# Cross-attention and experts, two layers: x stays in SBUF, the experts' outputs are added to it by one accumulating transfer per group

## What is computed

```python
# layer 0 (all matrices float32)
x = x + tanh(g_xattn[0]) * attention0(layernorm(x), ctx, mask)     # 16 heads of 8
n = layernorm(x)
e = argmax(n @ Wg.T)                                               # one of 8 experts
y = gelu(n @ W1[e] + b1[e]) @ W2[e] + b2[e]                        # 128 -> 512 -> 128
x = x + tanh(g_ffn[0]) * y
# layer 1
x = x + tanh(g_xattn[1]) * attention1(layernorm(x), ctx)           # no mask
x = x + tanh(g_ffn[1]) * top2_of_16_experts(layernorm(x))          # capacity 8 per sequence
```

## Time and profile before

| | us |
|---|---|
| median of 3 runs | 517.33 |
| lowest and highest | 516.51 and 517.77 |
| the profiled execution: time | 514.45 |
| the profiled execution: span from first to last instruction | 512.4 |

### The profile page before, as it was taken

How to read it: one execution, slowest core, us unless ns; L and a number is a source line. 1 busy time by engine, 2 the same in 40 slices (tenths; PEclk the granted TensorE clock), 3 DMA queues, 4 the chain that set the end, 5 groups by cost and what they waited for, 6 DMA issues and landing times.

```text
span 512.4 us, 21949 instructions
## 1 busy us (share of the span) xinstructions
PE 443.6 (87%) x8481; PEld 324.1 (63%) x8481; DVE 349.9 (68%) x883; ACT 320.6 (63%) x764; POOL 272.6 (53%) x325
## 2 busy tenths in 40 slices
PE   2789999999988796999998799998998697779996
PEld 1456676666655685999973466666665565445554
DVE  5578778888768665545532678888898677644545
ACT  2355566666865873677744466777777377685653
POOL 2622634646466178888886445553545236534454
PEclk9999999999999998999999799999999899898999
DMA  7124444232111155565436000110031000000112
GB/s 209 51 55 130 98 127 125 82 95 70 44 55 35 35 139 90 82 89 71 44 35 155 2 25 24 45 35 24 4 95 26 21 4 3 2 2 5 42 53 68
DMA packets 50629, 30.69 MB, mean 60 GB/s; under 512 B 12384, under 2 KB 46944, under 8 KB 50528
## 3 DMA queue, kind: packets, MB, share of 16 engines
q1 hardware_dynamic: 37072, 18.54, 13.7%
q0 software_dynamic: 6640, 4.67, 7.2%
q10 hardware_dynamic: 6816, 6.08, 4.3%
HBM read 19.42 MB, written 9.85 MB: 57 GB/s over the span
## 4 chain that ended last, share of the span: by engine, by line
PE 49%; DVE 20%; issue 13%; ACT 7%; POOL 4%; DMA 3%; ACTq 1%; DVEq 1%; SPq 0%; POOLq 0%
PE T_ps L865 8%; DVE maxes L600 7%; PE S_ps L854 6%; DVE prob L608 4%; PE A_ps L880 4%; PE f_H_ps L1199 3%; PE m_H_ps L1458 3%; PE f_Y_ps L1213 3%; PE S_ps L848 3%; PE Q_ps L835 2%; PE m_X_ps L1485 2%; PE m_T_ps L1498 2%; PE Q_ps L747 2%; PE m_X_ps L1469 2%; PE X_ps L897 2%
## 5 line engine op out<-in xcount | busy, mean ns | idle before, releaser
L600 DVE TENSOR_REDUCE maxes<-S_ps 128x16 f32<-128x1024 f32 x64 | 78.2, 1222 | 49.1 <-PE S_ps L854 49.0
L428 POOL TENSOR_TENSOR k_blk<-kT,col_a 128x512 f32<-128x512 f32 x64 | 67.7, 1067 | 79.4 <-ACT kT L489 54.0
L531 ACT ACTIVATE probT<-T_ps 128x512 f32<-128x512 f32 x128 | 76.0, 594 | 46.4 <-PE T_ps L865 45.6
L865 PE MATMUL T_ps<-col_a,prob 128*128 128x128 f32 x512 | 83.8, 287 | 15.1 <-DVE prob L608 11.3
L865 PEld LDWEIGHTS T_ps<-col_a,prob 128*128 128x128 f32 x512 | 56.5, 143 | 55.4 <-issue 29.9
L608 DVE TENSOR_TENSOR prob<-S_ps,maxes 128x512 f32<-128x512 f32 x128 | 82.5, 686 | 2.2
L1147 POOL DMA_INDIRECT x_mid<-f_out,f_rows x39 | 60.9, 1562 | 11.9 <-issue 9.2
L880 PE MATMUL A_ps<-v_blk,probT 128*32 128x18 f32 x4096 | 48.8, 187 | 0.1
L1012 DVE TENSOR_TENSOR f_hid<-f_H_ps,f_b 128x512 f32<-128x512 f32 x39 | 27.0, 692 | 31.5 <-PE f_Y_ps L1213 28.1
L880 PEld LDWEIGHTS A_ps<-v_blk,probT 128*32 128x32 f32 x4096 | 42.2, 111 | 9.5 <-issue 8.7
L854 PE MATMUL S_ps<-k_blk,qT 32*64 32x256 f32 x1024 | 46.9, 410 | 0.9 <-ACT qT L525 0.3
(11 more groups left out here) (199 smaller groups left out, 868.5 us busy)
## 6 DMA issues: line engine op xcount, KB each, us to landing
f_w<-in_W ACTq DMA_DIRECT2D x16, 256.0 KB, 3.0
ctxT<-in_ctxT SPq DMA_DIRECT2D x12, 256.0 KB, 3.0
f_rows<-sorted_rows SPq DMA_DIRECT2D x39, 64.5 KB, 2.1
out<-m_final SPq DMA_DIRECT2D x32, 64.0 KB, 1.5
x_all<-in_x SPq DMA_DIRECT2D x6, 256.0 KB, 5.7
x_mid<-x_all SPq DMA_DIRECT2D x6, 256.0 KB, 3.1
x_all<-x_mid SPq DMA_DIRECT2D x6, 256.0 KB, 3.5
ctxT<-in_ctxT SPq DMA_DIRECT2D x8, 128.0 KB, 2.7
```

The lines of the kernel that those rows point to most:

```text
L428: nc.gpsimd.tensor_tensor(k_blk[:, t % 2, :, :, :], kT[:, g.at(R), t - g.first, :].rearrange("p (b k) -> p b k", b=2).unsqueeze(2).to_broa ...
L531: nc.scalar.activation(probT[:, t % 2, 4 * h:4 * h + 4, :], T_ps[:, :, :], ACT.Exp, scale=SCALE).then_inc(probT_ready, 1)
L600: nc.vector.tensor_reduce(maxes[:, t % 2, :, :], S_all[:, :, 0:HQ * S].rearrange("p r (e k) -> p r e k", k=S), X, ALU.max).then_inc(max_re ...
L865: last = nc.tensor.transpose(T_ps[:, j, :], pair, ident[:, :])
```

## The change

x is not written to DRAM any more: `keep` and the loads of layer 1 are gone, and so are the waits on them. `f_out` and `f_hid` get SBUF of their own, and `f_hid` three buffers instead of two (`HIDS`). `send` writes its rows plainly, without an add, to a tensor `y_mid`; since each token is in one expert, each row is written once. The token numbers (`ids`) are changed so that row p·32 + t of `y_mid` belongs to partition p of tile t, which makes a group's outputs one contiguous piece per partition. A new step on POOL, `raise_x`, adds a group's piece of `y_mid` to `x_all` by one accumulating transfer; DVE's statistics of layer 1 wait for it (`y_in`). For the first two groups it stands ahead of `blocks` in `gpsimd_ahead`, and the first one waits for all sends; for the others it is at `head(-13)`.

```diff
             def load_x(g):
...
-                from_ = dram["x"] if masked else r["x_mid"]
-                sp.dma_start(x_group(g), from_[dram_rows(g), :].rearrange("(u p) d -> p u d", p=P)).then_inc(x_in[g.at(4)], 16)
+                sp.dma_start(x_group(g), dram["x"][dram_rows(g), :].rearrange("(u p) d -> p u d", p=P)).then_inc(x_in[g.own % 4], 16)
...
-            def keep(g):
-                sp.wait_ge(y_added, g.i + 1)
-                sp.dma_start(r["x_mid"][dram_rows(g), :].rearrange("(u p) d -> p u d", p=P), x_group(g)).then_inc(kept[g.own >= FULL_GROUPS], 16)
...
-            steps = [(load_x, groups, head(-13)), (load_ctx, late, head(-12))]
+            steps = [(load_ctx, late, head(-12))]
             if masked:
-                steps += [(load_mask, groups, head(-11)), (keep, groups, tail(5))]
+                steps = [(load_x, groups, head(-13))] + steps + [(load_mask, groups, head(-11))]
...
+            def raise_x(g):
+                if g.own == 0:
+                    for k, s in enumerate(r["y_sent"]):
+                        pool.wait_ge(s, 16 * ((MAX_TILES - k + len(r["y_sent"]) - 1) // len(r["y_sent"])))
+                pool.wait_ge(ln_stats, units_to(g.i - 4))
+                pool.dma_start(x_all[:, g.local * D:(g.local + g.n) * D],
+                               r["y_mid"][0:B * S, :].rearrange("(p t) d -> p (t d)", p=P)[:, g.local * D:(g.local + g.n) * D],
+                               accum_op=ALU.add).then_inc(y_in[g.own % 4], 16)
...
         def gpsimd_ahead(pool):
+            blocks, raise_x = gpsimd_steps(pool)
+            for g in groups[:2]:
+                raise_x(g)
             for t in tiles[:2]:
-                gpsimd_steps(pool)(t)
+                blocks(t)
...
-                steps += [(gaps, groups, settled(7, 11, short, later))]
+                steps += [(gaps, groups, settled(7, 11, short, later)), (raise_x, groups[2:], head(-13))]
...
             def stat(u):
                 g = u.group
-                dve.wait_ge(x_in[g.at(4)], 16 * (g.i // 4 + 1))
+                dve.wait_ge((x_in if masked else y_in)[g.own % 4], 16 * (g.own // 4 + 1))
...
+    HIDS = 3
...
-    out = r["over_x"].take("f0_out", [P, DEEP, D])
-    hid = r["over_x"].take("f0_hid", [P, 2, NC0, P])
+    out = sb("out", [P, DEEP, D])
+    hid = sb("hid", [P, HIDS, NC0, P])
...
         def bias(t):
...
-            if t == 0:
-                dve.wait_ge(done["kept"][0], 16 * FULL_GROUPS)
             dve.wait_ge(hidden, t + 1)
-            wait(dve, y_ready, t - 1)
+            wait(dve, y_ready, t - HIDS + 1)
...
     def sync(sp):
...
-        all_sent(sp)
...
         def send(t):
-            if t == 0:
-                pool.wait_ge(done["kept"][0], 16 * FULL_GROUPS)
-            if t == FULL_TILES:
-                pool.wait_ge(done["kept"][1], 16 * (NG - FULL_GROUPS))
...
-            pool.indirect_dma_start(r["x_mid"], bass.IndirectOffsetOnAxis(ap=rows[:, t % RINGS, D:RW].bitcast(I32), axis=0),
-                                    out[:, t % DEEP, :], None, compute_op=ALU.add).then_inc(sent[t % DEEP], 16)
+            pool.indirect_dma_start(r["y_mid"], bass.IndirectOffsetOnAxis(ap=rows[:, t % RINGS, D:RW].bitcast(I32), axis=0),
+                                    out[:, t % DEEP, :], None).then_inc(sent[t % DEEP], 16)
...
-    arrays["ids"] = (np.arange(NT + PADS)[None, :] * P + p[:, None]).astype(np.int32)
+    tile = np.arange(NT + PADS)[None, :]
+    arrays["ids"] = np.where(tile < NT, p[:, None] * NT + tile, tile * P + p[:, None]).astype(np.int32)
```

More of the change, by code:

```diff
@@ L253, in attention @@
     x_in = [sem(f"x_in{k}") for k in range(4)]
+    y_in = [sem(f"y_in{k}") for k in range(4)]
     ctx_loaded = [sem(f"ctx_loaded{k}") for k in range(CR)]
     mask_loaded = [sem(f"mask_loaded{k}") for k in range(R)]
-    kept = [sem("kept_full"), sem("kept_rest")]
     mask_made = sem("mask_made")
@@ L310, in attention @@
     x_banks = {}
-    done = {"row_written": rows_ready, "scattered": scattered, "kept": kept, "slots_known": slots_known, "raised_done": raised_done, "summed": summed,
+    done = {"row_written": rows_ready, "scattered": scattered, "slots_known": slots_known, "raised_done": raised_done, "summed": summed,
             "shifted": shifted, "probT_ready": probT_ready, "y_added": y_added, "r_xn_ready": r_xn_ready,
@@ L403, in load_mask @@
                              dram["mask"][dram_rows(g), :].rearrange("(u p) k -> p u k", p=P)).then_inc(mask_loaded[g.at(R)], 16)
-            def keep(g):
-                sp.wait_ge(y_added, g.i + 1)
-                sp.dma_start(r["x_mid"][dram_rows(g), :].rearrange("(u p) d -> p u d", p=P), x_group(g)).then_inc(kept[g.own >= FULL_GROUPS], 16)
-            return load_x, load_ctx, load_mask, keep
+            return load_x, load_ctx, load_mask
         def sync_ahead(sp):
@@ L414, in sync @@
         def sync(sp):
-            load_x, load_ctx, load_mask, keep = sync_steps(sp)
-            steps = [(load_x, groups, head(-13)), (load_ctx, late, head(-12))]
+            load_x, load_ctx, load_mask = sync_steps(sp)
+            steps = [(load_ctx, late, head(-12))]
             if masked:
-                steps += [(load_mask, groups, head(-11)), (keep, groups, tail(5))]
+                steps = [(load_x, groups, head(-13))] + steps + [(load_mask, groups, head(-11))]
             run(steps + hook["sync"](sp))
@@ L472, in gaps @@
                 nc.gpsimd.tensor_tensor(r["gap"][:, at], r["top"][:, at, 1], r["top"][:, at, 0], ALU.subtract).then_inc(gap_ready, 1)
-            blocks = gpsimd_steps(pool)
+            blocks, raise_x = gpsimd_steps(pool)
             steps = [(blocks, tiles if masked else tiles[2:], shift(-2)), (norm, groups, head(-10)), (r_norm, groups, settled(3, 6, short, later))]
@@ L977, in experts0 @@
     y_out = sem("y_out")
-    sent = [sem(f"sent{k}") for k in range(DEEP)]
+    sent = r["y_sent"]
+    assert len(sent) == DEEP
     vec, act, pe = nc.vector, nc.scalar, nc.tensor
@@ L998, in staggered @@
                     step(n - skew)
-    def all_sent(eng):
-        for k in range(DEEP):
-            eng.wait_ge(sent[k], 16 * ((MAX_TILES - k + DEEP - 1) // DEEP))
     def tile_vector(dve):
@@ L1007, in bias @@
             e = dve.value_load(entry(1, t), min_val=0, max_val=E0 - 1)
[L1008 to L1009 removed]
             dve.wait_ge(hidden, t + 1)
[L1011 to L1012 removed]
+            wait(dve, y_ready, t - HIDS + 1)
+            vec.tensor_tensor(hid[:, t % HIDS, :, :], H_ps[t % 2][:, :, :],
                               b1[:, bass.ds(e, 1), :].rearrange("p a c -> p (a c)").unsqueeze(2).to_broadcast([P, NC0, P]),
@@ L1169, in gelu @@
             eng.wait_ge(biased, t + 1)
-            act.activation(hid[:, t % 2, :, :], hid[:, t % 2, :, :], ACT.Gelu).then_inc(gelu_done, 1)
+            act.activation(hid[:, t % HIDS, :, :], hid[:, t % HIDS, :, :], ACT.Gelu).then_inc(gelu_done, 1)
         return [(gelu, 3), (weights, 0)], [(turn_out, 0)]
@@ L1212, in down @@
             for n in range(NC0):
-                last = pe.matmul(Y_ps[t % 2][:, 0:D], hid[:, t % 2, n, :],
+                last = pe.matmul(Y_ps[t % 2][:, 0:D], hid[:, t % HIDS, n, :],
                                  w2[:, bass.ds(e, 1), n, :].rearrange("p a c -> p (a c)"),
@@ L1580, in program @@
         shared = {"sorted": nc.dram_tensor("sorted_rows", (ROWS, RW), F32, kind="Internal").ap(),
-                  "x_mid": nc.dram_tensor("x_mid", (B * S + PADS * P, D), F32, kind="Internal").ap(),
+                  "y_mid": nc.dram_tensor("y_mid", (B * S + PADS * P, D), F32, kind="Internal").ap(),
+                  "y_sent": [sem(f"f0_sent{k}") for k in range(4)],
                   "bias_ready": sem("bias_ready"), "ids_ready": sem("ids_ready"), "pads_ready": sem("pads_ready"), "scaled": sem("scaled"),
@@ L1586, in program @@
         r1.update(shared)
-        r0["over_x"] = over_x
         r0["reach"] = sb("reach", [P, E0, NT])
```

4 lines of the change are left out of this document (1 added, 3 removed).

## The result

| | before | change |
|---|---|---|
| median of 4 executions each, us | 516.92 | 525.87 |
| ratio, with its 95% interval | | 1.0174 (1.0129 to 1.0219) |
| profiled execution: time / span, us | 514.45 / 512.4 | 523.76 / 522.0 |

The change costs 9 us; forecast were 5.5. Two later series of the same kernel gave 1.0123 (1.0058 to 1.0188) and 1.0194 (1.0131 to 1.0256). Executions of one kernel differ by several us, and those with a lower mean granted clock are mostly the longer ones; so beside whole times I compare stages, which repeat far better. Ratios and counts of executions leave out those that are over 1.5% above the fastest of their series (the profiled ones of e5 and e6 are of these).

The account below looks back on a forecast made before the run. PE bounds the experts' stage, but draining and a DVE-POOL ladder bound the hand-over. Two landings there outweigh the sends' 3.4 us gain: first maximum 5.5 us later, carried in full, 517.33 to 522.8 us; range 518.7 to 526.4.

Parts of the forecast that it names:

- The ladder's terms: Hand-over, POOL's norm of group 10 to DVE's first maximum: two landings in a row, 6.15 + 2L = 13.95 us, not 7.28.
- G: Time one accumulating transfer holds POOL: put at 1.25 us, between ends of 0.46 and 1.56.
- L: Time from a four-tile transfer's issue to its landing (256 KB): put at 3.9 us, between 2.2 and 5.4.
- 2G + 2L − 4.8: General shift of layer 1's first row maximum at the hand-over: 5.5 us later with the chosen prices.
- POOL has no backlog at the end: End of the experts' stage: plain sends at 1.3 us per tile stay under PE's pace; last send at 265.9.
- The gain of the plain sends: Draining at the hand-over: all sends landed at 268.9 instead of 272.3, a gain of 3.4 us.
- The rule on the price: Skill page's transfer from GpSimd: about 2.0 us plus bytes at 436 GB/s; 2.6 us for 256 KB, shift +2.9 us.
- Carried to the end: Layer 1's maxima, subtractions and PE's transposes wait behind DVE's statistics, so the 5.5 us reach the end in full.
- The other six transfers cost nothing: Later transfers between k_blk's on a mostly idle POOL: no cost; without that cover 9.3 us at most.
- Third buffer, removed writes, shorter sends inside the stage at no price: Experts' stage: all three hidden behind a PE without gaps, so removing or changing them gains nothing.
- The rival that the experts' stage shortens: Waits on f_Y or sends bind PE somewhere: 2.2 us back, time 520.5; chance 0.06.
- The clock rival: PE's low-clock stretch after the longer wait becomes twice as long: 3.0 us more, 525.7; chance 0.10.

Follow-up runs that it names:

- e5: The changed kernel run again as it is, with more repetitions: ratio 1.0123 (1.0058 to 1.0188).
- e6: The changed kernel with transfers that write x_all without adding, x left out: ratio 1.0054 (1.0001 to 1.0107).
- e1: The changed kernel with the transfers of groups 12 and 13 issued together with those of 10 and 11, ahead of k_blk: 1.0031 (0.9996 to 1.0065) of before.
- e9: The kernel before with SP's x loads of groups 12 and 13 waiting for POOL's norms of groups 10 and 12: ratio 1.0095 (1.0050 to 1.0139).
- e4: The kernel before with plain indirect sends instead of adding ones, the addition of x left out: ratio 0.9933 (0.9898 to 0.9968).
- e3: The kernel before with the second k_blk of layer 1 done eight times, a mere delay: ratio 1.0094 (1.0046 to 1.0142).
- e8: The changed kernel with SP loading outputs of groups 10 to 13, DVE adding them to x, and k_blk first on POOL: 0.9997 (0.9953 to 1.0040) of before.
- e10: The changed kernel run once more as it is, to see the time at 1.2 GHz: ratio 1.0194 (1.0131 to 1.0256).
- e2: The changed kernel with four transfers issued together and the two k_blk put ahead of them: 1.0044 (0.9998 to 1.0089) of before.
- e7: The changed kernel with two hidden buffers instead of three: ratio 1.0152 (1.0061 to 1.0243).

## Why the prediction was right, and what was off

**Mechanism and sign: right.** The place that was to decide, two landings one behind the other between POOL's norms and DVE's statistics, is where the time went. It is shown from both sides: taking the order away gives 6.0 us back (e1), and putting the order alone into the kernel before costs 3.0 us of hand-over (e9). Its time is 4.9 us (2.6 to 7.2) longer by the ratio and 2.7 by the medians; what the former has beyond 3.0 isn't explained.

**The ladder's terms.** G was put at 1.25 and is 0.95, L at 3.9 and is 4.2. That the formula 2G + 2L − 4.8 gives 5.5 with either pair is luck: the two errors cancel. The hand-over grew by 23.82 − 17.13 = 6.7, which is 1.2 more. From the norm of group 10 to the first maximum 13.95 was forecast, and 286.92 − 272.63 = 14.29 measured, 0.34 more. The other 0.86 lie ahead of it, and there the step that failed is "POOL has no backlog at the end" and the landing behind it. The last three outputs come 0.89 and 1.05 us apart, faster than a send every 1.26, so the last send starts 1.14 us after the last f_out, not 0.57; POOL then starts the first transfer 267.87 − 264.24 = 3.63 us after it, not 3.1. So the first transfer is 1.1 us later than forecast. The trace of before showed this already: its last three outputs are 0.84 and 1.12 us apart, the last two in the earlier trace rows, and ahead of them

```profile
263.37 0.29 DVE L1023 TENSOR_TENSOR f_out<-f_Y_ps,f_b 128x128 f32<-128x128 f32 x1
```

The shorter G gives back only a part of the 1.1 us, because the norm of group 10 starts 0.78 us after the k_blk, when the landing of group 10 has let the statistics through, and not right behind them. The gain of the plain sends, put at 3.4, is 2.7 (e4).

**The rule on the price.** Without adding, 256 KB land after 3.0 us; with it after 4.2. The rule of the Trainium skill, page "DMA: Bandwidth & Descriptors", section on the anatomy of one DMA on the gpsimd path, gave an estimate of 2.6 us, near the first and 1.6 under the second; its sum of +2.9 us would have been nearer to e6 (+3.7 at the hand-over) than to the change (+6.7).

**Carried to the end: nearly.** e3 turned 5.2 us of delay into 4.8 (2.4 to 7.3), an interval that leaves room for less. In the change 0.8 of the 6.7 us come back by the tenth maximum, and 5.9 are left (59.06 against 53.19 from the last f_out).

**"The other six transfers cost nothing": right within 1 us.** Only the first four of the ten kept DVE waiting (who waited for L432, us in all, times):

```profile
  DVE stats L640: 16.9, 4
```

From the tenth maximum to the end, before, e3, e4 and e9 take 192.6 to 194.0 us, and the kernels with transfers at best 194.9 (e8, e10). The least difference, 0.9, has the size of a stall that was not foreseen. PE stops inside one group of 64 matmuls, in the change as in e1, e2, e5, e7, e8 and e10:

```profile
322.79 0.69 PE L887 MATMUL A_ps<-v_blk,probT 128*32 128x18 f32 x59
324.66 0.25 PE L887 MATMUL A_ps<-v_blk,probT 128*32 128x18 f32 x5 [1.18 <-issue]
```

In e6 the same group runs through:

```profile
323.21 0.74 PE L886 MATMUL A_ps<-v_blk,probT 128*32 128x18 f32 x64
```

No instruction or landing releases it, and its cause is open. There is a lead: in all seven a 16 KB transfer of the queue that the page calls "instruction" (q8) ended 0.1 to 0.4 us before the stall began, and in e6 one ended 0.8 us before the whole group. Where the last piece takes 197 to 200 us, more of it ran at 1.2 GHz: 16 to 31 us (e2, e5, e6, e1, change) against 8 to 12 in the other seven.

**Third buffer, removed writes, shorter sends inside the stage at no price: right as far as the runs go.** e7 shows it for the buffer, e4's last f_out at 268.3 for the sends; for the writes there is only PE at 10.00 of 10. The rival that the experts' stage shortens seemed to come true in the first profile, by 2.2 us, and fell with the repeats.

**The clock rival: not where it was put.** It put 3.0 us on a low stretch twice as long right after the wait. From the first to the tenth maximum the granted clock is 0.91 before and 0.92, 0.90 and 0.91 in the three profiles of the change, and this piece is no longer (35.2 to 35.8 us against 36.06). What is new is low clock inside the hand-over, 0.91, 0.87 and 0.85 against 1.00 before, with no price that can be seen: e7 has 0.95 there and the longest hand-over. Of the 9 us, 5.9 are the hand-over and 0.9 to 1.2 the stall. That leaves some 2 us, and the clock is the only other difference found; in the first profile of the change the last piece alone is 5.9 us longer than before, with 31 us of it at 1.2 GHz against 10. Whether the change brings that or chance does is open. So what was forecast, and rightly, is the hand-over; the rest of the 9 us is within the range by luck.

**Slips.** Three of the prediction's sums are 0.1 us or so low: 518.7 for 517.33 + 1.5, 525.7 for 522.8 + 3.0, and 520.5 for 522.8 − 2.2. Nothing hangs on them.

## What to carry to other kernels

When a load moves into the queue of an engine that also computes, look first at what it stands behind: four landings overlap when their transfers are issued together, and add up when each is issued behind work that needs the landing before it. Issue what the first steps of a stage need before that stage's own ladder begins, and put work that is ready anyway into the wait ahead of it. When executions scatter more than the effect, compare stages between two fixed instructions; here they repeat within 0.4 us while spans differ by 2.6.

## What the runs showed of the hardware that was not expected

- An add in a transfer from POOL costs on both sides. A transfer holds POOL for 0.95 us in the mean, and one of 256 KB lands after 4.2 us; without the add it is 0.61 and 3.0 us; an indirect send of 128 rows takes 1.56 us of POOL with the add and 0.95 without.
- Transfers issued back to back overlap: in e1 four of them, issued from 270.19 on, let DVE take the statistics of the first group at 274.27 and of the third at 277.41. Each may land later than alone: there the longest landing took 6.7 us, in the change 4.5.
- The granted clock of the same kernel lay between 0.951 and 0.990 over 56 executions, with no change in the program.
